# Macaron block on one core: the low part of the input layer's product is taken on VectorE out of PSUM, with five PSUM banks for the feed-forward layers and new places for the attention steps

## The reference

```python
x = x + 0.5 * ffn(layernorm(x))
x = x + attention(layernorm(x))
x = x + 0.5 * ffn(layernorm(x))
```

## Time and profile before

| | |
|---|---|
| runs | 1532.97, 1529.48, 1532.85 us; median 1532.85 us |
| profiled execution | 1529.28 us, span 1527.4 us |
| PE | 1472.4 us busy (96%), 6914 matmuls |
| DVE | 1025.6 us (67%) |
| ACT | 679.3 us (44%) |
| POOL | 572.1 us (37%) |
| mean granted PE clock | 0.994 |

### The profile page before, as it was taken

The page is one execution under the profiler, slowest core; times in us unless marked ns, Lnnn a source line. Parts: engine busy times, 40 slices in busy tenths (PEclk is TensorE's granted clock), DMA queues, the critical chain, the costliest instruction groups (busy, mean ns, idle before and its releaser), DMA issues.

```text
span 1527.4 us, 19080 instructions
## 1 busy us (share of the span) xinstructions
PE 1472.4 (96%) x6914; PEld 1207.8 (79%) x6914; DVE 1025.6 (67%) x1349; ACT 679.3 (44%) x1063; POOL 572.1 (37%) x466
## 2 busy tenths in 40 slices
PE   6989999999999999999899999899999999989998
PEld 5777878787877788878687878788888878778887
DVE  6524777875867677859684978596577777872322
ACT  7653545343535344444353534435344444343532
POOL 3011263462462436251735170807225345353100
PEclk9999999999999999999999999999999999999999
DMA  8765668766575775858656777585675867854332
GB/s 297 274 244 172 208 215 319 245 236 214 193 258 180 253 275 188 279 173 288 234 182 209 264 243 249 186 288 177 218 251 179 287 226 235 285 194 145 103 118 71
DMA packets 189347, 338.21 MB, mean 221 GB/s; under 512 B 15680, under 2 KB 138688, under 8 KB 188864
## 3 DMA queue, kind: packets, MB, share of 16 engines
q1 hardware_dynamic: 189248, 336.93, 64.4%
HBM read 314.85 MB, written 30.41 MB: 226 GB/s over the span
## 4 chain that ended last, share of the span: by engine, by line
PE 83%; POOL 5%; DVE 4%; DMA 3%; ACT 3%; issue 2%; SPq 0%; DVEq 0%; POOLq 0%; ACTq 0%
PE f_bank L1155 27%; PE f_bank L1156 27%; PE a_banks L1230 7%; PE f_bank L1115 6%; PE f_bank L1116 6%; PE f_bank L1184 3%; PE f_bank L1185 3%; PE a_banks L1250 2%; POOL acc L773 2%; DMA weights_hi<-in_ffn_w 2%; DVE slot L1026 1%; DMA slot<-keys_and_values 1%; POOL h_lo L787 1%; PE f_bank L1103 1%; DVE slot L1070 1%
## 5 line engine op out<-in xcount | busy, mean ns | idle before, releaser
L1155 PE MATMUL f_bank<-h_hi,wring 128*128 128x512 f32 x2048 | 810.9, 396 | 8.0 <-DMA wring<-weights_hi 3.8
L1156 PE MATMUL f_bank<-h_lo,wring 128*128 128x512 f32 x2048 | 799.6, 390 | 0.0
L1155 PEld LDWEIGHTS f_bank<-h_hi,wring 128*128 128x128 f32 x2048 | 385.6, 188 | 92.1 <-DVE h_lo L926 4.7
L1156 PEld LDWEIGHTS f_bank<-h_lo,wring 128*128 128x128 f32 x2048 | 385.8, 188 | 80.9 <-issue 2.2
L856 ACT ACTIVATE h_hi<-f_bank,colv 128x512 fp32r<-128x512 f32 x256 | 176.4, 689 | 544.5 <-PE f_bank L1156 544.2
L926 DVE TENSOR_TENSOR h_lo<-f_bank,h_hi 128x512 fp32r<-128x512 f32 x256 | 175.8, 687 | 250.2 <-ACT f_bank L857 249.1
L787 POOL TENSOR_TENSOR h_lo<-f_gated,h_hi 128x512 fp32r<-128x512 f32 x128 | 170.3, 1343 | 348.0 <-ACT h_hi L850 347.5
L1115 PE MATMUL f_bank<-fT_hi,w_in 128*128 128x512 f32 x512 | 205.8, 402 | 9.2 <-ACT f_gated L845 3.8
L1116 PE MATMUL f_bank<-fT_lo,w_in 128*128 128x512 f32 x512 | 200.9, 392 | 0.0
L1026 DVE TENSOR_TENSOR slot<-slot,a_banks 128x1280 f32<-128x1280 f32 (+4 forms) x124 | 170.6, 1376 | 16.3 <-DMA slot<-keys_and_values 16.2
L1032 DVE TENSOR_REDUCE S<-slot 128x80 f32<-128x1280 f32 (+4 forms) x124 | 171.7, 1385 | 4.3
(11 more groups left out here) (115 smaller groups left out, 1141.4 us busy)
## 6 DMA issues: line engine op xcount, KB each, us to landing
wring<-weights_hi SPq DMA_DIRECT2D x248, 512.0 KB, 4.8
slot<-keys_and_values SPq DMA_DIRECT2D x128, 384.0 KB, 4.6
slot<-keys_and_values SPq DMA_DIRECT2D x64, 640.0 KB, 4.3
slot<-keys_and_values SPq DMA_DIRECT2D x312, 128.0 KB, 4.5
slot<-keys_and_values SPq DMA_DIRECT2D x64, 256.0 KB, 5.6
weights_hi<-in_ffn_w SPq DMA_DIRECT2D x16, 512.0 KB, 6.8
keys_and_values<-kv_out SPq DMA_DIRECT2D x32, 256.0 KB, 3.2
slot<-in_ffn_w SPq DMA_DIRECT2D x10, 512.0 KB, 5.3
```

The lines of the kernel that those rows point to most:

```text
L1155: pe.matmul(bank[:, :], hi, h_hi[src][:, k, :], start=(k == 0), stop=False)
L1156: last = pe.matmul(bank[:, :], hi, h_lo[src][:, k, :], start=False, stop=(not general and k == KH - 1))
```

## The change

- `f_gate` writes the product back into the w2 bank in PSUM instead of `f_gated`. `f_cut` on ACT reads it there. `f_low` is now a DVE instruction that reads the bank and `h_hi`. POOL no longer has it. Silu of step m waits for `f_gate` (not `f_low`) of step m-3.
- A w2 bank is now empty only when `f_low` has run.
- The feed-forward layers have five banks after the opening (four in it). The fifth is the second half of the attention pair that held `p_banks`. The softmax weights of row block 0 now lie in `q_bank`, and block 1's share `p_bank` with z and the output product. The exponentials of block 0 so no longer wait for the last residual. A query projection now waits for the previous subtile's softmax sums and its weighted values of block 0.
- Most numbers of `TIMES`, `FOLLOW`, `OPENING` and `STARTS` differ.

```diff
-TIMES = [3.65, 9.56, 11.46, 12.91, 17.19, 25.44, 22.37, 3.94, 7.13, 53.75, 61.23, 3.2, 93.09, 4.73]
+TIMES = [3.97, 9.03, 11.34, 17.27, 17.92, 25.33, 22.96, 3.78, 8.05, 53.33, 61.23, 3.21, 93.33, 4.89]
...
-        t_bank, q_bank, *p_banks = [pair[:, n * 512:(n + 1) * 512] for pair in pairs for n in range(2)]
+        t_bank, q_bank, p_bank, fifth = [pair[:, n * 512:(n + 1) * 512] for pair in pairs for n in range(2)]
+        fb.append(fifth)
...
+        for steps, banks in (opening(), 4), (timeline()[0], 5):
...
+                    bank = len(bank_of) % banks
+                    bank_of[use], used_before[use], last_use[bank] = bank, last_use.get(bank), use
...
             if name == "f_in":
                 m, w = rest
-                return r.marks.prod if w else r.marks.silu, r.of("input", m + 1)
+                return r.marks.low if w else r.marks.silu, r.of("input", m + 1)
...
-            def f_low_(r, m):
-                pool.wait_ge(r.marks.phi, r.of("input", m + 1))
-                pool.tensor_tensor(h_lo[r.p][:, m, :], f_gated[:, m % 3, :], h_hi[r.p][:, m, :].bitcast(fp32),
-                                   ALU.subtract).then_inc(r.marks.low, 1)
...
-                    act.wait_ge(r.marks.low, r.of("input", m - 2))
+                    act.wait_ge(r.marks.prod, r.of("input", m - 2))
...
-                act.activation(h_hi[r.p][:, m, :], f_gated[:, m % 3, :], ACT.Copy).then_inc(r.marks.phi, 1)
+                act.activation(h_hi[r.p][:, m, :], f_bank("f_in", r, m, 1)[:, :], ACT.Copy).then_inc(r.marks.phi, 1)
...
-                dve.scalar_tensor_tensor(g, u[:, :], scale_col(1, m), g, ALU.mult, ALU.mult).then_inc(r.marks.prod, 1)
+                dve.scalar_tensor_tensor(u[:, :], u[:, :], scale_col(1, m), g, ALU.mult, ALU.mult).then_inc(r.marks.prod, 1)
+
+            def f_low(r, m):
+                dve.wait_ge(r.marks.phi, r.of("input", m + 1))
+                dve.tensor_tensor(h_lo[r.p][:, m, :], f_bank("f_in", r, m, 1)[:, :], h_hi[r.p][:, m, :].bitcast(fp32),
+                                  ALU.subtract).then_inc(r.marks.low, 1)
...
                 elif what == "q":
-                    after(pe, a_qk, qk_before(a))
+                    if a.i:
+
+                        before = subs[a.i - 1]
+                        pe.wait_ge(a_sum, before.at(1, 1))
+                        pe.wait_ge(a_pv, per_group.at(before, sum(n == 0 for n, g in groups_of[before.c])))
```

More of the change, by code:

```diff
@@ L31 @@
          "z", "out"]
-TIMES = [3.65, 9.56, 11.46, 12.91, 17.19, 25.44, 22.37, 3.94, 7.13, 53.75, 61.23, 3.2, 93.09, 4.73]
-FOLLOW = dict(silu=-1.5, gate=-0.08, cut=1.63, low=1.99, gelu=-0.77,
-              lo=1.12, residual=-0.87, store=2.93, fill=23.53, stats=-0.47, turn=4)
-OPENING = dict(block=9.27, block_step=1.86, compare=2.04, turn=8.2, input=13.0, count=52.85)
-STARTS = [50.0, 118.7, 184.3, 274.4, 343.7, 411.3, 489.6, 575.0,
-          642.8, 722.6, 789.0, 867.0, 962.9, 1038.6, 1110.1, 1179.0]
+TIMES = [3.97, 9.03, 11.34, 17.27, 17.92, 25.33, 22.96, 3.78, 8.05, 53.33, 61.23, 3.21, 93.33, 4.89]
+FOLLOW = dict(silu=-1.38, gate=-0.05, cut=0.51, low=1.83, gelu=-0.57,
+              lo=1.67, residual=0.34, store=3.36, fill=25.31, stats=-0.47, turn=4)
+OPENING = dict(block=8.49, block_step=1.81, compare=0.98, turn=8.83, input=12.92, count=49.3)
+STARTS = [50.0, 118.7, 184.5, 270.9, 344.9, 423.4, 492.1, 574.0,
+          636.0, 704.4, 782.2, 866.8, 960.6, 1043.4, 1107.4, 1178.9]
 class Counts:
@@ L500, in key @@
             return (name, r.j, *rest)
-        uses = []
-        for name, (r, *rest) in [*pe_steps(opening()), *pe_steps(timeline()[0])]:
-            uses += [key(name, r, *rest, w) for w in range(2)] if name == "f_in" else [key(name, r, *rest)]
-        use_of = {use: i for i, use in enumerate(uses)}
+        bank_of, used_before, last_use = {}, {}, {}
+        for steps, banks in (opening(), 4), (timeline()[0], 5):
+            for name, (r, *rest) in pe_steps(steps):
+                for use in [key(name, r, *rest, w) for w in range(2)] if name == "f_in" else [key(name, r, *rest)]:
+                    bank = len(bank_of) % banks
+                    bank_of[use], used_before[use], last_use[bank] = bank, last_use.get(bank), use
         def f_bank(name, r, *rest):
-            return fb[use_of[key(name, r, *rest)] % 4]
+            return fb[bank_of[key(name, r, *rest)]]
         def counted(name, j, *rest, attempt):
@@ L783, in a_add @@
                     pool.tensor_tensor(z[:, n, :], z[:, n, :], acc[:, 4, :], ALU.add).then_inc(a_acc, 1)
-            def f_low_(r, m):
-                pool.wait_ge(r.marks.phi, r.of("input", m + 1))
-                pool.tensor_tensor(h_lo[r.p][:, m, :], f_gated[:, m % 3, :], h_hi[r.p][:, m, :].bitcast(fp32),
-                                   ALU.subtract).then_inc(r.marks.low, 1)
-            schedule({"f_rstd": f_rstd_, "f_low": f_low_}, opening())
-            pool.wait_ge(s_flag, 1)
-            has_lo = pool.value_load(flag[0:1, 0:1])
-            with pool.If(has_lo != 0):
-                schedule({"f_low": f_low_}, beginning(begins[1], 0.0))
-            schedule({"f_rstd": f_rstd_, "f_low": f_low_, "a_rstd": a_rstd_, "a_bout": a_bout_, "a_add": a_add},
-                     timeline()[0])
+            schedule({"f_rstd": f_rstd_}, opening())
+            schedule({"f_rstd": f_rstd_, "a_rstd": a_rstd_, "a_bout": a_bout_, "a_add": a_add}, timeline()[0])
         @block.scalar
@@ L983, in _ @@
                         cut_block(it, s, True)
[L984 removed]
+                schedule({"f_gate": f_gate, "f_low": f_low, "f_lo": f_lo_}, beginning(begins[1], 0.0))
             def f_residual(r, n):
```

25 lines of the change are left out of this document (11 added, 14 removed).

## The result

The changed kernel takes **1544.36 us** (median of 5 runs, 1540.23 to 1545.72) against 1531.2 us for the kernel before beside it (5 runs, 1528.38 to 1532.97). The ratio is **1.0091**, 95% interval 1.0073 to 1.0108: slower by 13 to 14 us. The forecast was 1542 us. The profiled execution took 1545.27 us with a span of 1543.4, which is 16.0 us over the profiled execution of before. The forecast for that one was +9, so seven microseconds have to be found.

What follows compares the result with a forecast made beforehand. PE, busy for 1472.4 of 1527.4 us, was taken as the bound. The terms +24 - 7 - 3 - 4 - 2 + 2 - 1 gave +9 us, on the median of 1532.85 us 1542 us, range 1537.5 to 1551.

Steps and rivals of the forecast that it cites:

- The new waits of the input phases: Input phases: PE waits 33.6 us in sum for DVE's later low parts, less about 9.5 before; net +24 us.
- (a): Attention projections (kv0) no longer wait behind their own transposes in six of ten places: -7 us, between -4 and -10.
- (b): The one wait of a hidden step for POOL's `f_low` goes: -3 us.
- (c): Transposes' waits for `a_hat` shrink, as `a_rstd` no longer queues behind `f_low` on POOL: -4 us, between -7 and +3.
- (d): Waits for z in attention: DVE is later, but PE too; -2 us, between -4 and +4.
- The clock: PE at half clock after long waits: +5 us in passes 3, 5, 14, two old places vanish; net +2, -3 to +6.
- The opening: Before pass 1: DVE's added lows are offset by shorter compares and gaps, its sum still in time; -1 us, -2 to +3.
- the signs: Changed profile: `f_low` 0.68 to 0.70 us, `h_lo` waits 20 to 35, `aT` 2 to 4, POOL near 400, DVE near 1110.
- the first (smaller new waits): Input phases: new waits smaller than the old ones that go, `f_low` waits under about 20 us; 1521 us, chance 0.22.
- The second, a balance: Input phases: new waits sum to 26 instead of 33.6 us, gains as forecast; about 1533 us, chance 0.2.
- The third (DVE the bound outside the input phases too): DVE's backlog reaches hidden layers: z +4, `a_hat` +3, three worst passes 2 us more each, clock +3; 1558 us, chance 0.15.
- The fourth, a wait of q for its bank: Shared bank: q waits some 3 us for block 0's weighing in two or three subtiles; about 1550 us, chance 0.03 alone.

Runs made afterwards that it cites:

- the split of two passes: Against the kernel before, at its old places: five banks, low part on DVE in passes 5 and 10 alone; 1521.94 us, 0.9938.

## Why the prediction was right, and where not

The direction and the mechanism hold, and the size in the main. The forecast was +9 us and the measured difference is 13 to 14. That 1542 comes within 3 us of 1544.36 is in part luck: the forecast stood on a median of 1532.85, and the one beside the changed kernel is 1531.2. And the terms miss in both directions, the opening and the clock one way, z and the DMA waits the other. To compare term by term, I take the start-to-start time of PE's matmuls over the usual one of their kind. It sums to 62.7 us before and 79.0 after (16.3 more, the spans differ by 16.0), and holds waits, slow restarts and half clock.

**The new waits of the input phases: +24 net, measured +25.0.** Bank and residual waits with their restarts are 8.9 us before (the forecast took 9.5 for these) and 33.9 after, without the opening. By pass, the waits were forecast and measured: pass 3, 7.9 and 7.9; pass 4, 5.9 and 6.5; pass 5, 3.7 and 3.6; pass 13, 6.1 and 6.3; pass 14, 4.4 and 4.3. Pass 9 has 0 for 1.3. Of the nine passes that were put at 4.3 together, pass 7 was missed: forecast at most 0.8, measured 3.8, while the other eight have 1.6. So the sum came out right with help from errors that cancel. Pass 7:

```profile
705.30 0.68 DVE L1011 TENSOR_TENSOR gate<-a_banks,rowv 128x512 f32<-128x512 f32 x1
705.90 0.75 DVE L927 SCALAR_TENSOR_TENSOR f_bank<-f_bank,colv,f_gated 128x512 f32<-128x512 f32 x1
706.56 1.48 DVE L1023 TENSOR_TENSOR slot<-slot,a_banks 128x1280 f32<-128x1280 f32 x1
708.07 1.49 DVE L1029 TENSOR_REDUCE S<-slot 128x80 f32<-128x1280 f32 x1
709.47 0.75 DVE L927 SCALAR_TENSOR_TENSOR a_banks<-a_banks,colv,f_gated 128x512 f32<-128x512 f32 x1
710.13 0.68 DVE L931 TENSOR_TENSOR h_lo<-f_bank,h_hi 128x512 fp32r<-128x512 f32 x1
```

There PE's attention work makes the phase long on average, which I took for slack, but a pair and an eviction of the attention gate stand right ahead of one low part. In pass 4 the sum was near and its parts were not: 2.70 us (2.87 with the restart) of the 6.5 are a wait for a *hidden* layer's low part at the third input step, and the first output half, for which the prediction worked out a wait of 2.4 us, waited 0.70. The late low part stands behind score pairs that DVE ran without a break from 379.07 us on, after 3.30 us of idle time for rows of the DMA. So it isn't work that pass 3's input phase had left over.

**What goes.** (a) `aT`: -7 forecast, -7.5 measured. (b) POOL: -3 and -3.2. (c) `a_hat`: -4 and -3.1. (d) z: -2 and -5.8 with `zT`. This comes from the new places and not from where the low part is made: at the new places no kernel, with GpSimd's or DVE's low part, has more than 0.6 us of waits for z, but for the one with the low part right behind the cut (2.5), and those at the old ones have 1.3 to 4.1. (e) The DMA waits were to stay unchanged; they fell by 2.1 us. That POOL's lighter queue makes the shorter way to the transposes bearable, as I argued, is shown by three runs: 16.6 and 17.6 us of waits with GpSimd's subtractions at the new places, 3.8 without them.

**The clock: +2 forecast, +4.1 measured.** This is what PE's matmuls lost in the stretches of granted half clock (1.2 of 2.4 GHz), over their usual start-to-start time and without the waits: 6.8 us before, 10.9 after. The granted clock behind six waits (first column the stretch, then its length, PE and the rest as in the earlier trace rows; the clock is the number ahead of the last two):

```profile
500.60:503.70 3.10, 3.09 (x8) 2.47 (x9) 2.60 (x3) 1.10 (x3) 0.00 (x0) 0.52 0.01 3
303.60:306.70 3.10, 3.09 (x26) 3.09 (x27) 3.06 (x4) 0.60 (x1) 0.00 (x0) 1.00 0.84 235
397.80:400.90 3.10, 3.10 (x7) 2.47 (x8) 3.10 (x4) 1.60 (x3) 0.00 (x0) 0.50 0.83 260
710.90:714.00 3.10, 3.10 (x10) 2.48 (x11) 3.07 (x4) 1.18 (x2) 0.00 (x0) 0.64 0.59 199
1281.90:1285.00 3.10, 3.05 (x7) 2.48 (x8) 3.03 (x6) 0.97 (x3) 0.00 (x0) 0.50 0.51 162
1367.80:1374.00 6.20, 6.20 (x21) 5.43 (x22) 4.83 (x7) 1.86 (x4) 0.00 (x0) 0.50 0.07 27
```

Five of them, behind waits of 3.39, 2.70, 3.67, 2.19 and 3.39 us, run at or near the lower level of 1.2 GHz. Four lose 1.5 to 1.7 us on top of the wait, and the last one, where the half clock lasts twice as long, 2.9. I had counted three such places (passes 3, 5 and 14) and two of before as gone. Three of before went, passes 4, 7 and 13 came without having been counted, and pass 3 has none. The prediction's comparison of 3.71 and 5.40 us also had a reading slightly wrong: the wait before the faster twelve records was 0.69 us and not 0.9.

**The opening: -1 forecast, +3.7 measured** (the start of pass 1). This is the step that failed: "DVE gets 5.5 us of lows", of which "eight at the short length give back 3.4, and DVE had some 3 us of gaps". I weighed DVE's work in sum and asked if its last result came in time. It did (DVE's sum at 57.88 us, PE's count at 61.45), and it was not what PE waited for. I had worked out for the five banks which low part each step needs, and never did it for the opening's four, where every step from the third on needs one. The compares did come down from 1.65 to 1.22 us throughout, and DVE's sum came at 57.88 instead of 55.22 all the same. The relief was also put too high: before, only five of the compares beside the input steps were long (one of 2.00 us and four of 1.64 or 1.65), which gives 2.5 us and not 3.4. The Trainium skill ("SBUF — State Buffer", Who interferes with whom) gave the reason for the relief, and the trace agrees with it: 1.66 us beside GpSimd's subtractions, 1.22 without. By that rule alone the opening would have gained.

**What the terms add up to.** 25.0 - 7.5 - 3.2 - 3.1 - 5.8 + 4.1, and +3.6 for the waits of the opening, -2.1 for those on the DMA and +1.0 for low parts inside the hidden layers, are 12.0 of the 16.3 us. The other 4.3 are spread in small pieces over matmuls outside these waits and stretches, and no run shows what they come from.

**Of the signs** that the prediction named, most hold (684 ns, 28.3 us of waits, `aT` at 3.2, POOL at 403). DVE is at 1095 us and not near 1110.

**Of the rivals**, the first (smaller new waits) decides at 20 us of waits for `f_low`; there are 28.3. The second, a balance with new waits of 26 us, fails too: they are 33.9. The third (DVE the bound outside the input phases too) did not come: the waits for z vanished. (Its own items add up to 1560 us or more and not 1558.) The fourth, a wait of q for its bank, is in no trace.

**Where the 0.9% lies**, by runs, all against the kernel before:

| step | ratio | part |
|---|---|---|
| kernel before | 1.0000 | |
| with a fifth bank | 0.9969 | -0.31% |
| and the new places | 1.0019 | +0.50% |
| and the low part on DVE in nine passes (split kernel) | 0.9916 | -1.03% |
| and in passes 3, 4, 5, 7, 13, 14 | 1.0057 | +1.41% |
| and in the opening (the changed kernel) | 1.0091 | +0.34% |

The interval of each ratio is 0.1 to 0.2% to either side, so a part, as a difference of two, is known to 0.2 or 0.3%. So the change holds a gain of 13 us that is given back twice: 22 us in six input phases in which DVE had no room, 5 us in an opening with four banks and a full DVE. That the move pays only where DVE has room is shown by the 1.41% of the six passes. Whether it needs the new places as well is not shown: the nine-pass split was not run at the old ones, and the split of two passes that was run there comes to 0.9938.

## What to carry to other kernels

When an instruction moves to another engine and a buffer's release moves with it, do two sums, per place and not on average: what the new engine has to do between this buffer's fill and its release, and which use needs the buffer next; and redo the second for every stretch in which the number of buffers differs. If the sums differ from place to place, split the work by place: here nine of sixteen passes had it on VectorE and seven on GpSimd, and the split beat both pure forms at the new places (a split of two passes only just did at the old). (Which side each single pass is better on was not tried.) A table of places tuned for one form is worth little for the other (it was worth 1.5% to one and cost the other 0.5 to 0.8%), so compare forms with their own tables as well as with each other's.
